# Three edits at once in a latent-attention kernel: ScalarE's order in a loop, the loads of its keys, and the end of a stage

## The chip, the cores and the metric

The kernel runs on one core of a Trainium2 chip. The metric is the device time of one execution in microseconds (us). A core has five engines that run side by side and meet at semaphores: TensorE (PE, matmuls, with its weight loads shown as PEld), VectorE (DVE), ScalarE (ACT), GpSimd (POOL) and SyncE (SP, which here only issues DMAs). Sixteen DMA engines move data between HBM and the core's memory.

## What is computed

Two layers over a small state x (128 tokens of 256 numbers) and a long context `ctx_1024` (12544 tokens of 256 numbers), each of an attention over or fed by the context, an attention among the tokens and a feed-forward part:

```python
x = x + _L0_xattn_ref(_layernorm(x), ctx_1024, ...)   # the "history"
x = x + _L0_attn_ref(_layernorm(x), ...)
x = x + _L0_ffn_ref(_layernorm(x), ...)               # 16 experts, top 2, and a shared one
x = x + _L1_xattn_ref(_layernorm(x), ctx_1024, ctx_1024, ...)
x = x + _L1_attn_ref(_layernorm(x), ...)
x = x + _L1_ffn_ref(_layernorm(x), ...)
```

Two of them see the context, and the change touches only these:

```python
# _L0_xattn_ref: the history is pooled to one vector, from which convolution kernels are made
eh = _gelu(_ln(historical_data @ hist_W + hist_b, hist_ln_g, hist_ln_b))
aw = softmax(_gelu(eh @ ctx_W1 + ctx_b1) @ ctx_W2 + ctx_b2, axis=1)
cc = jnp.sum(eh * aw, axis=1)
kp = _gelu(_ln(cc @ kg_W1 + kg_b1, kg_ln_g, kg_ln_b)) @ kg_W2 + kg_b2
# _L1_xattn_ref: 16 heads of 16 numbers; keys and values are the context times Wq
scores = jnp.einsum('blhe,bshe->bhls', qp, kp)
attn = jax.nn.softmax(scale * scores, axis=-1)
out = jnp.einsum('bhls,bshd->blhd', attn, vp)
```

## The kernel before, in words

**History loop (some 20 to 403 us).** The context goes through in 49 chunks of 256 tokens (`NCH`, `CH`). Each engine runs its own loop over the chunks n, in an order written out by hand; semaphores join them. For chunk n TensorE (loop behind L724) does in turn: the first half of the product with `hist_W` (`project(n, 0)`, L647), the mean square of chunk n - 1 (L673), the transposes of the keys n - 1 for the values (`values_turn`, L722), the second half of the product, the spreading of chunk n - 1's deviations over all rows (`spread_rstd`, L681), in odd chunks a logit product (L705), a half of the hidden product (L696), and the key product of chunk n (`keys_product`, L647, into bank 7). Products with 32-bit data are split in high and low parts.

ScalarE (loop at L1279) does in chunk n: in odd n the hidden's Gelu (`hide_act`, L1216), the key's copy with bias into `k_full` for n - 1 (`keys_full`, L1253), the squares of the first half (`squares(n, 0)`, L1231), the high part of the input n + 1 (`high_part`, L1210), the values' copy (`values_copy`, L1263), the copy of the spread deviations (`widen`, L1238), `squares(n, 1)`, and two features, Gelu with scale and bias (`features`, L1223). In n = 15, 23, 31, 39 and 47 the exponentials of a finished group (`weights`, L1244, group = (n - 15) / 8) take the place of the features; the two features left over come in the next chunk, ahead of its own two (`group_before`, `feature_pair`). Exponentials and Gelu are of different tables of ScalarE; what changes a table is an ACT_TABLE_LOAD. Copies and squares need none.

VectorE makes the high and low parts of the keys (`keys_parts`), adds squares, normalises, and forms the weighted sums. SyncE stores keys and values to HBM: `k_scratch` is an array of 2 (high, low) by 256 by 12544 numbers.

**The history's end (some 403 to 444 us).** VectorE works through the last weighted sums, forms the pooled vector and spreads it (`cc_wide`, L1659). Then it waits until all keys and values are stored, and sets `history_done` (L1664): the memory of the history may now be written over. ScalarE waits for it ahead of `kT` and `v0` (L1318), SyncE ahead of the loads of `rows0` and the experts' weights. VectorE then builds `q_blocks` (L1687), and takes the layer statistics of the product `kg1`. TensorE: the turn of `xn1`, the products to `qkv0`, `kg1` (five products on `cc_wide`), the 16 scores on `q_blocks` and `kT` (L797), the transpose of `kg_h` (L803).

`stay_awake(n, bank)` (L759) is n products of the identity with itself, the results of which nobody reads.

**The context attention (some 548 to 870 us).** Eight pairs of heads s, each with 25 units of 512 keys. `k_stack[s % 2]` holds the keys of a pair: for each head hh of the two, at rows 64 hh: 16 rows high, 16 rows low, one row of ones, 16 rows high. TensorE first finds each unit's maxima (`maximum`, L985; it waits for the chunk's loads), some 28 units ahead of the scores (L1009) and the sums over the values (L1024); VectorE reduces the maxima (L1893), ScalarE takes the exponentials (L1401). The keys come by `load_keys(s, c)` on SyncE's queue in 7 chunks of 1792 keys, six DMAs each, of 16 rows of 7168 bytes. The queue's order: after `x1` two loads of a row of ones (L611) and the keys of pair 0; after `x3` the values of pair 0, ones, the keys and values of pair 1; then for each pair keys and values, a chunk as soon as the scores of pair s - 2 are through with it.

Of the kernel before, what the change touches and what calls it, by code (L numbers as in the profile page):

```python
# [19 lines left out]
F32 = mybir.dt.float32  # L20
# [12 lines left out]
HD = D // H  # L33
# [146 lines left out]
DVE_STEPS = """  # L180
hist_constants hist_weights x_parts mask var1 xn1 g_shift cc_wide history_done q_blocks0 var_kg kg_n att0_0 att0_1
kg_hT att0_2 att0_3 kern_shift kernels s_max0 s_max2 s_max1 probT0 s_max3 probT1
# [83 lines left out]
def build_kernel(nc, k_scratch, v_scratch, ones_scratch, ctx_t, x_in, mask_in, const_in, hist_in, l0_in, rows0_in, xw_in, x_bo_in, x_o_in, l1_in, rows1_in, v_in,  # L266
                 tables_in, out):
    with ExitStack() as outer:
# [265 lines left out]
        def _(sp):  # L534
# [54 lines left out]
            def load_keys(s, c):  # L589

                cols = slice(c * CHUNK, (c + 1) * CHUNK)
                if s >= 2:
                    sp.wait_ge(c_sc, exp_at[EU * (s - 2) + ((c + 1) * CHUNK - 1) // UK][0] + 1)
                for at, which in ((0, 0), (HD, 1), (2 * HD + 1, 0)):
                    for hh in range(2):
                        row = 2 * HD * s + HD * hh
                        sp.dma_start(k_stack[s % 2][64 * hh + at:64 * hh + at + HD, cols].bitcast(F32),
                                     k_scratch[which, row:row + HD, cols]).then_inc(c_stack[s % 2][c], 16)

# [43 lines left out]
        def _(pe):  # L643
# [134 lines left out]
            pe.wait_ge(ld_l0, 16 * L0_PIECES)  # L778
            pe.wait_ge(h_nm, CT * NCH)
            turn("xn1", xn, "xn1_t")  # L780
            act_s.wait(pe, "xT1")
# [6 lines left out]

            pe.wait_ge(ld_kg, 16)
            dve_s.wait(pe, "cc_wide")  # L790
            kg1, kg2 = part(w0, L0_COLS, "kg1", CT), part(w0, L0_COLS, "kg2", KD)
# [183 lines left out]
            def maximum(m):  # L975
# [6 lines left out]
                if u == 0 or (hi - 1) // CHUNK > (lo - 1) // CHUNK:  # L982
                    pe.wait_ge(c_stack[s % 2][(hi - 1) // CHUNK], 96 * (s // 2 + 1))
                for hh, at in enumerate(max_banks(m)):
# [205 lines left out]
        def _(act):  # L1190
# [44 lines left out]
            def widen(n):  # L1235
                act.wait_ge(h_bc, n + 1)
                wait_at(act, h_nm, CT * n)
                A(rstd_wide[:, :], bank[:, 4, 0:CH], ACT.Copy).then_inc(h_rw, 1)  # L1238
# [40 lines left out]
            for n in range(NCH):  # L1279
                if n % 2 == 1 and 0 <= (n - 7) // 2:  # L1280
                    hide_act((n - 7) // 2)
                if 1 <= n:
                    keys_full(n - 1)
                squares(n, 0)
                if 1 <= n and n + 1 < NCH:
                    high_part(n + 1)
                if 1 <= n:
                    values_copy(n - 1)
                    widen(n - 1)
                squares(n, 1)  # L1290
                if group_before(n - 1) is not None:
                    feature_pair(n - 1)
                if group_before(n) is not None:
                    weights(group_before(n))
                else:
                    feature_pair(n)
# [197 lines left out]
        def _(dve):  # L1494
# [164 lines left out]
            done(V.tensor_copy(cc_wide[:, :, :], cc[:, :].unsqueeze(2).broadcast_to([P, CT, P])), "cc_wide")  # L1659
            for b in range(2):  # L1660
                dve.wait_ge(k_stored[b], 32 * ((NCH + 1 - b) // 2))
                dve.wait_ge(v_stored[b], 16 * ((VG + 1 - b) // 2))
            dve.wait_ge(pe_s.sem, 1)
            done(V.memset(gone[:, :], 0.0), "history_done")  # L1664

# [33 lines left out]
            head_blocks(q_blocks, bank[:, 1, 0:T], 0)  # L1699
            head_blocks(q_blocks, bank[:, 1, T:2 * T], 1, "q_blocks0")  # L1700
            pe_s.wait(dve, "kg1")
            layer_stats("_kg", bank[:, 0, 0:D])
# [356 lines left out]
```

## Time and profile before

| | us |
|---|---|
| timed runs | 928.0, 930.33, 933.86 (median 930.33) |
| the profiled execution | 921.35 |
| its span, first to last instruction | 919.6 |
| TensorE busy | 853.1 |
| VectorE busy | 632.9 |
| ScalarE busy | 549.5 |

The profile is of one execution, with a time of its own. The span is what its rows are told in; around it lie 1.75 us. A row of a timeline has the start, the duration, the engine, the line of the kernel, the operation, what it writes and reads, and in brackets how long the engine had stood still and who released it.

### The profile page before, as it was taken

What the parts mean: (1) busy time and instruction counts of PE and PEld (TensorE: products, weight loads), DVE (VectorE), ACT (ScalarE), POOL (GpSimd) and SP (SyncE); (2) the same over time, 40 slices, a digit from 0 to 9 for tenths busy, and PEclk for the clock granted to TensorE, in tenths of its full rate; (3) what the DMA queues carried; (4) which work ended last, traced back from release to release, by engine and by line L of the source; (5) the groups of instructions that cost most, each with busy time, mean ns of one, the idle gap of its engine ahead of it and who ended that gap; (6) DMA issues with size and microseconds to landing.
All of it is one profiled execution on the core that took longest, in us unless ns stands there. A gap on an engine that the chain in (4) does not pass through costs nothing. (4 is left out here: it accounts for less than half of the span.)

```text
span 919.6 us, 21802 instructions
## 1 busy us (share of the span) xinstructions
PE 853.1 (93%) x8804; PEld 690.0 (75%) x8804; DVE 632.9 (69%) x1289; ACT 549.5 (60%) x947; POOL 104.1 (11%) x116
## 2 busy tenths in 40 slices
PE   3999999999999999995889989999999999999988
PEld 3988888887878878864686963677777777778776
DVE  3555666676767767778883449997799999892253
ACT  1776777687686786783731110465577777677521
POOL 1322222222222222200000000000000000000000
PEclk9999999999999999996999999998799999999988
DMA  3376365456546635607608559479698999925100
GB/s 126 105 165 174 106 178 145 140 135 159 144 139 152 150 107 144 164 24 149 278 1 133 83 135 174 116 131 192 118 206 199 163 213 201 156 88 172 62 1 7
DMA packets 83141, 125.01 MB, mean 136 GB/s; under 512 B 10776, under 2 KB 73498, under 8 KB 82268
## 3 DMA queue, kind: packets, MB, share of 16 engines
q1 hardware_dynamic: 83040, 123.61, 56.6%
q8 instruction: 70, 1.15, 0.6%
q14 instruction: 31, 0.25, 0.1%
HBM read 84.06 MB, written 39.52 MB: 134 GB/s over the span
## 5 line engine op out<-in xcount | busy, mean ns | idle before, releaser
L1893 DVE TENSOR_REDUCE unit_max<-bank 128x1 f32<-128x512 f32 (+1 forms) x350 | 221.2, 675 | 29.3 <-PE bank L985 27.6
L1401 ACT ACTIVATE prob<-bank 128x1024 f32<-128x1024 f32 (+1 forms) x200 | 190.8, 1005 | 84.5 <-PE bank L1009 83.9
L647 PE MATMUL bank<-hc_high,w_high 128*128 128x256 f32 x392 | 117.6, 300 | 8.6 <-POOL hc_low L1461 8.4
L1558 DVE SCALAR_TENSOR_TENSOR normed<-bank,b_centered,rstd_wide 128x256 f32<-128x256 f32 x196 | 85.4, 477 | 48.3 <-ACT rstd_wide L1238 48.1
L1024 PE MATMUL bank<-prob,vals 128*32 128x128 f32 x3136 | 110.8, 281 | 3.8 <-issue 2.7
L1009 PEld LDWEIGHTS bank<-q_stack,k_stack 49*128 49x128 f32 x1568 | 105.2, 192 | 11.0 <-ACT q_stack L1393 3.2
L647 PE MATMUL bank<-hc_high,w_low 128*128 128x256 f32 x392 | 112.9, 288 | 0.0
L647 PE MATMUL bank<-hc_low,w_high 128*128 128x256 f32 x392 | 112.6, 287 | 0.0
L1009 PE MATMUL bank<-q_stack,k_stack 49*128 49x128 f32 x1568 | 105.3, 272 | 2.3 <-ACT q_stack L1393 1.1
L985 PE MATMUL bank<-k_stack,q_max 49*128 49x512 f32 (+1 forms) x400 | 100.9, 498 | 2.8 <-DVE unit_max L1893 2.7
L1024 PEld LDWEIGHTS bank<-prob,vals 128*32 128x32 f32 x3136 | 82.4, 112 | 26.9 <-issue 21.9
L1231 ACT ACTIVATE square<-bank,b_centered 128x256 f32<-128x256 f32 x196 | 82.0, 472 | 28.8 <-PE bank L647 28.8
L696 PE MATMUL bank<-eh,hw 128*128 128x512 f32 (+1 forms) x200 | 92.2, 585 | 0.5 <-ACT eh L1223 0.5
L647 PEld LDWEIGHTS bank<-hc_high,w_high 128*128 128x128 f32 x392 | 76.6, 195 | 9.4 <-issue 9.4
L647 PEld LDWEIGHTS bank<-hc_high,w_low 128*128 128x128 f32 x392 | 76.8, 196 | 0.0
L647 PEld LDWEIGHTS bank<-hc_low,w_high 128*128 128x128 f32 x392 | 76.4, 195 | 0.0
L1223 ACT ACTIVATE eh<-normed,hw 128x512 f32<-128x512 f32 (+1 forms) x100 | 74.5, 806 | 0.1
L647 PE MATMUL bank<-hc_high,x_high 128*128 128x256 f32 x196 | 73.2, 373 | 0.0
L985 PEld LDWEIGHTS bank<-k_stack,q_max 49*128 49x128 f32 x400 | 38.3, 187 | 42.9 <-DVE unit_max L1893 19.5
L1582 DVE CUSTOM_DVE_ANT_0 eh<-eh,logits 128x1024 f32<-128x1024 f32 (+1 forms) x52 | 59.5, 1161 | 14.7 <-POOL h_rstd L1466 12.9
L1461 POOL TENSOR_TENSOR hc_low<-hc_raw,hc_high 128x512 fp32r<-128x512 f32 x49 | 62.5, 1275 | 46.4 <-DVE group_stats L1582 45.2
L1536 DVE CAST k_high<-k_full 128x512 fp32r<-128x512 f32 x49 | 20.9, 426 | 64.6 <-ACT k_full L1253 62.5
(324 smaller groups left out, 1339.2 us busy)
## 6 DMA issues: line engine op xcount, KB each, us to landing
k_stack<-k_scratch SPq DMA_DIRECT2D x336, 112.0 KB, 5.4
vals<-v_scratch SPq DMA_DIRECT2D x8, 1666.0 KB, 9.0
v_scratch<-vst SPq DMA_DIRECT2D x12, 1088.0 KB, 10.2
hc_raw<-in_ctx_t SPq DMA_DIRECT2D x49, 256.0 KB, 3.1
k_scratch<-k_high SPq DMA_DIRECT2D x49, 256.0 KB, 3.4
k_scratch<-k_low SPq DMA_DIRECT2D x49, 256.0 KB, 3.5
w_ffn<-in_l SPq DMA_DIRECT2D x4, 1920.0 KB, 14.0
w_l<-in_l SPq DMA_DIRECT2D x6, 603.0 KB, 5.6
```

The lines of the kernel that those rows point to most:

```text
L647: last = nc.tensor.matmul(out_ap, lhs, rhs, start=(n == 0), stop=(n == len(pairs) - 1))
L696: last = nc.tensor.matmul(bank[:, w1_bank(i), 0:width], w1_hist[:, c, :], eh[:, gb, c, at:at + width], start=(c == 0), stop=(c == CT - 1))
L985: last = nc.tensor.matmul(bank[:, at, 0:hi - lo], q_max[head_rows[hh], s, :], k_stack[s % 2][head_rows[hh], lo:hi], start=True, stop=True)
L1009: last = nc.tensor.matmul(bank[:, at + hh, t * T:(t + 1) * T], k_stack[s % 2][head_rows[hh], k * P:(k + 1) * P], q_stack[head_rows[hh], s, ...
L1024: last = nc.tensor.matmul(bank[at:at + 32, SUM_BANK, 0:T], vals[:, s % 2, hh, k * VW:k * VW + 32], prob[:, e % NPB, hh, t * T:(t + 1) * T] ...
L1223: A(eh[:, group % 2, c, at:at + width], normed[:, i % 2, c, 0:width], ACT.Gelu, bias=v_hist["beta"][:, c:c + 1], scale=v_hist["g"][:, c:c ...
L1231: ins = A(square[:, c, :], bank[:, 2 * (n % 2) + half, (c % 2) * CH:(c % 2 + 1) * CH], ACT.Square, bias=b_centered[:, c:c + 1])
L1401: A(prob[:, e % NPB, :, 0:width], bank[:, at:at + 2, 0:width], ACT.Exp).then_inc(c_exp, 1)
L1461: TT(hc_low[:, b], hc_raw[:, b], hc_high[:, b].bitcast(F32), ALU.subtract).then_inc(h_low, 1)
L1558: V.scalar_tensor_tensor(out=normed[:, n // 2 % 2, c, at:at + CH], in0=bank[:, 2 * b + half, (c % 2) * CH:(c % 2 + 1) * CH], scalar=b_cent ...
L1582: V.tensor_tensor_reduce(part_of, part_of, logits[:, gb, lo:lo + width], 1.0, 0.0, ALU.mult, ALU.add, group_stats[:, group, half * CT + c: ...
L1893: V.tensor_reduce(unit_max[:, s % 2, u, hh:hh + 1], bank[:, at[hh], 0:width], AX_X, ALU.max, negate=True).then_inc(c_red, 1)
```

## The change

ScalarE's order in the two iterations behind the exponentials, and where the Gelu's table is loaded. In the first of them (`one_past`) a Gelu of one column comes before `widen`, and `keys_full(n)` of the chunk itself comes between the left-over and the own features. In the second (`two_past`) the values' copy, the high part and `widen` come before both squares, and `keys_full(n)` again before the features. So the two following iterations begin without their `keys_full`:

```diff
-                if 1 <= n:
+                one_past, two_past = (group_before(n - past) is not None for past in (1, 2))
+                if 1 <= n and group_before(n - 2) is None and group_before(n - 3) is None:
                     keys_full(n - 1)
-                squares(n, 0)
-                if 1 <= n and n + 1 < NCH:
-                    high_part(n + 1)
-                if 1 <= n:
+                if two_past:
                     values_copy(n - 1)
+                    if n + 1 < NCH:
+                        high_part(n + 1)
                     widen(n - 1)
+                    squares(n, 0)
+                else:
+                    squares(n, 0)
+                    if 1 <= n and n + 1 < NCH:
+                        high_part(n + 1)
+                    if 1 <= n:
+                        values_copy(n - 1)
+                        if one_past:
+                            A(table_now[:, :], ones[:, :], ACT.Gelu)
+                        widen(n - 1)
                 squares(n, 1)
-                if group_before(n - 1) is not None:
+                if one_past:
                     feature_pair(n - 1)
+                if n + 1 < NCH and (one_past or two_past):
+                    keys_full(n)
```

The keys' loads: for each head the high and low rows in one DMA of 32 rows, the second high rows in one of 16, so four DMAs a chunk. The wait on the chunk's semaphore counts 64 for 96:

```diff
-                for at, which in ((0, 0), (HD, 1), (2 * HD + 1, 0)):
+                for at, which in ((0, 2), (MAX_ROW + 1, 1)):
                     for hh in range(2):
-                        row = 2 * HD * s + HD * hh
-                        sp.dma_start(k_stack[s % 2][64 * hh + at:64 * hh + at + HD, cols].bitcast(F32),
-                                     k_scratch[which, row:row + HD, cols]).then_inc(c_stack[s % 2][c], 16)
+                        row, to = 2 * HD * s + HD * hh, 64 * hh + at
+                        sp.dma_start(k_stack[s % 2][to:to + which * HD, cols].bitcast(F32),
+                                     k_scratch[0:which, row:row + HD, cols]).then_inc(c_stack[s % 2][c], 16)
```

The history's end: VectorE sets `history_done`, with all its waits, behind `q_blocks0` rather than before, and TensorE gets identity products in two places:

```diff
             pe.wait_ge(h_nm, CT * NCH)
+            stay_awake(4, 4)
             turn("xn1", xn, "xn1_t")
...
             pe.wait_ge(ld_kg, 16)
+            stay_awake(8, 4)
             dve_s.wait(pe, "cc_wide")
```

## Rows read from the trace of the kernel before

**Rows 1.** The page, busy time of TensorE: us, share of the span, instructions.

```profile
PE 853.1 (93%) x8804; PEld 690.0 (75%) x8804; DVE 632.9 (69%) x1289; ACT 549.5 (60%) x947; POOL 104.1 (11%) x116
```

**Rows 2.** Waits: engine and line waited for, us in total, times, longest.

```profile
PE bank L722 <- ACT k_full L1253: 8.8, 6, 1.8
...
DVE gone L1664 <- DMA v_scratch<-vst: 1.7, 1, 1.7
```

**Rows 3.** Timeline of TensorE in the history loop, the products that spread deviations (start, duration).

```profile
136.25 0.61 PE L681 MATMUL bank<-const,h_rstd 128*128 128x128 f32 x4
...
146.81 0.85 PE L681 MATMUL bank<-const,h_rstd 128*128 128x128 f32 x4
...
155.21 0.60 PE L681 MATMUL bank<-const,h_rstd 128*128 128x128 f32 x4
...
162.48 0.61 PE L681 MATMUL bank<-const,h_rstd 128*128 128x128 f32 x4
...
330.66 0.61 PE L681 MATMUL bank<-const,h_rstd 128*128 128x128 f32 x4
...
341.09 0.99 PE L681 MATMUL bank<-const,h_rstd 128*128 128x128 f32 x4
```

**Rows 4.** Timeline of ScalarE and TensorE behind an exponential, and in the last chunk.

```profile
136.89 0.38 ACT L1238 ACTIVATE rstd_wide<-bank 128x256 f32<-128x256 f32 x1 [0.83 <-PE bank L681]
...
138.02 1.28 ACT L1223 ACT_TABLE_LOAD   x1
139.32 2.93 ACT L1223 ACTIVATE eh<-normed,hw 128x512 f32<-128x512 f32 x4
142.16 0.67 ACT L1216 ACTIVATE hidden<-bank,hw 128x512 f32<-128x512 f32 x1
142.73 0.82 ACT L1253 ACTIVATE k_full<-bank,x_wts 128x256 f32<-128x256 f32 x2
...
143.60 0.86 PE L722 MATMUL bank<-const,k_full 128*128 128x128 f32 x4 [1.82 <-ACT k_full L1253]
...
400.60 1.98 PE L696 MATMUL bank<-eh,hw 128*128 128x512 f32 x4 [0.54 <-ACT eh L1223]
```

**Rows 5.** Timeline of VectorE and TensorE at the history's end.

```profile
429.12 0.43 DVE L1659 COPY k_full<-cc 128x512 f32<-128x512 f32 x1
...
429.70 2.84 PE L647 MATMUL bank<-w_l,k_full 128*128 128x256 f32 x8 [2.20 <-DVE k_full L1659]
431.29 0.06 DVE L1664 MEMSET gone<- 128x1 f32 x1 [1.73 <-DMA v_scratch<-vst]
...
431.39 2.48 DVE L1687 TENSOR_TENSOR q_blocks<-bank,const 128x1024 f32<-128x1024 f32 x2
...
433.93 5.51 PE L797 MATMUL bank<-kT,q_blocks 128*128 128x128 f32 x32 [0.24 <-DVE q_blocks L1687]
...
439.27 0.38 PE L803 MATMUL bank<-const,kg_h 128*128 128x128 f32 x2
```

**Rows 6.** Windows: stretch, us, busy of each engine, then granted clock, DMA share, GB/s.

```profile
140.00:150.00 10.00, 8.18 (x44) 6.74 (x42) 4.81 (x12) 7.58 (x16) 1.96 (x2) 0.83 0.28 84
...
432.00:434.00 2.00, 1.76 (x5) 0.57 (x3) 1.93 (x3) 1.38 (x2) 0.00 (x0) 0.50 0.74 157
```

**Rows 7.** Windows while the experts' weights load, and while the first keys load.

```profile
436.00:450.00 14.00, 12.29 (x52) 7.58 (x50) 11.12 (x37) 7.52 (x14) 0.00 (x0) 0.95 1.00 426
...
490.00:500.00 10.00, 9.91 (x67) 7.70 (x66) 4.26 (x13) 2.40 (x4) 0.31 (x1) 1.00 1.04 155
```

**Rows 8.** Groups by line and shape: the identity products (busy us, mean ns, idle before).

```profile
L759 PE MATMUL bank<-const 128*128 128x128 f32 x278 | 39.6, 294 | 0.7 <-DVE xT L1941 0.7
```

**Rows 9.** DMA queue in 486.3 to 487.0 (packets, MB, share), SyncE's issue, and `k_stack`'s maxima.

```profile
q1 hardware_dynamic: 1, 0.05, 34.2%
...
485.60 0.54 SPq L611 DMA_DIRECT2D k_stack<-ones_scratch  x2
...
L985 PE MATMUL bank<-k_stack,q_max x400: 379/496/794, 547.8 to 831.6; 49*128 49x512 f32 x128, 49*128 49x256 f32 x6
```

More of the change, by code:

```diff
@@ L180 @@
 DVE_STEPS = """
-hist_constants hist_weights x_parts mask var1 xn1 g_shift cc_wide history_done q_blocks0 var_kg kg_n att0_0 att0_1
+hist_constants hist_weights x_parts mask var1 xn1 g_shift cc_wide q_blocks0 history_done var_kg kg_n att0_0 att0_1
 kg_hT att0_2 att0_3 kern_shift kernels s_max0 s_max2 s_max1 probT0 s_max3 probT1
@@ L982, in maximum @@
                 if u == 0 or (hi - 1) // CHUNK > (lo - 1) // CHUNK:
-                    pe.wait_ge(c_stack[s % 2][(hi - 1) // CHUNK], 96 * (s // 2 + 1))
+                    pe.wait_ge(c_stack[s % 2][(hi - 1) // CHUNK], 64 * (s // 2 + 1))
                 for hh, at in enumerate(max_banks(m)):
@@ L1659, in _ @@
             done(V.tensor_copy(cc_wide[:, :, :], cc[:, :].unsqueeze(2).broadcast_to([P, CT, P])), "cc_wide")
[L1660 to L1664, printed above, removed]
             def layer_stats(n, src):
@@ L1700, in _ @@
             head_blocks(q_blocks, bank[:, 1, T:2 * T], 1, "q_blocks0")
+            for b in range(2):
+                dve.wait_ge(k_stored[b], 32 * ((NCH + 1 - b) // 2))
+                dve.wait_ge(v_stored[b], 16 * ((VG + 1 - b) // 2))
+            dve.wait_ge(pe_s.sem, 1)
+            done(V.memset(gone[:, :], 0.0), "history_done")
             pe_s.wait(dve, "kg1")
```

## The prediction

> **What bounds the kernel now.** I read the page's first part, then the list of waits, then the timeline by stage. TensorE is busy for 93% of a span of 919.6 us [rows 1]: it is the bound, and time can only be won where it stands still, runs at half clock, or where another engine carries a serial stretch. The waits list [rows 2] names such a place in the history loop: the transposes of `k_full` (L722) wait for ScalarE 6 times, 8.8 us in all. The timeline shows where. The products that spread the deviations (L681) come once per chunk and mark its step, in turn 7.3 us (162.48 after 155.21) and 8.15 us (odd chunks also have a logit product). At 136.25 to 146.81 the step is 10.56 us, at 330.66 to 341.09 10.43 [rows 3]; four steps are long so, one behind each of the exponentials of groups 0 to 3 (10.56, 10.77, 9.38, 10.43; first and last shown). The cause is ScalarE's order [rows 4]: a table load of 1.28 us, four features of 2.93 us and the hidden of 0.67 us stand before the copy of `k_full` at 142.73, and TensorE idles 1.82 us for it. It then also drops to half clock (granted 0.83 in 140 to 150 [rows 6]).
>
> The second place is the history's end [rows 5]. VectorE ends the pooled context at 429.12 + 0.43 = 429.55, then `history_done` waits for the last value stores until 431.29, and only then come the two `q_blocks` products, 2.48 us, so that the scores start at 433.93 and the transpose of `kg_h` at 439.27. TensorE's clock is 0.50 in 432 to 434 [rows 6], that is 1.2 GHz, after it had stood still for 2.2 us ahead of 429.70.
>
> The third place does not show as a wait at all: the loads of the keys. No row has TensorE wait for `k_stack`. But the DMA share is 1.04 while they run, at only 155 GB/s; the weights get 426 GB/s at a share of 1.00 [rows 7]. So sixteen engines are full with them.
>
> **ScalarE's order.** In the iteration behind the exponentials the table load (through a one-column Gelu) moves ahead of `widen` (136.89), into its wait of 0.83 us: with the tiny Gelu's own time `widen` comes some 0.6 us late, which VectorE and TensorE have spare. `keys_full(n)` now comes behind two features, not behind four, the hidden and the load: from 142.73 go 0.67, two of the four features (1.46) and the 1.28 less the 0.6 lost, so it starts at some 139.9 and ends at 140.7. TensorE wants it at 143.60 - 1.82 = 141.8. In the next iteration the values' copy, the high part and `widen` come first and the squares after; the squares end some 2 us before the chunk's own key product, ScalarE waits for that with `keys_full` and the features queue behind it by that much; they are wanted two chunks on, so nobody waits. Each long step falls back to 7.29: 41.14 - 4 x 7.29 = 12.0 us; the steps behind them were 0.25, 0, 0.11 and 0.38 late as well. Sum 12.7 us. In the last iteration the load moves likewise, the features end earlier, and TensorE's wait of 0.54 us at 400.60 [rows 4] goes; I count 0.4, since the deviation from GpSimd is the next thing late. Bounds: -13.6 (every idle time of [rows 2] and every half-clock piece) and 0, if the wait only changes its name. The Trainium skill (ScalarE: Activation LUTs, What ACT_TABLE_LOAD costs) puts a table load with its drain at about 2.7 us; the row says 1.28, and that is what I use. By the page `widen` would be 2 us late, and the gain perhaps 1 us less for each.
>
> **The history's end.** `q_blocks` no longer waits for the stores: 429.55 + 2.48 = 432.1, then `history_done`, then ScalarE's `kT` 0.1 + 0.38 later at 432.6 (the stores at 431.29 are hidden behind `q_blocks`; what waits behind `history_done` is `kT`, `v0`, the layer statistics of `kg1` and, 0.8 us later than now in the stage, SyncE's loads of `rows0` and the expert weights, wanted 50 us later). The eight identity products run from 427.5, where `qkv0` ends, to some 429.8 (278 instructions for 139 products, 39.6 us: 0.285 us each [rows 8]) and keep the clock up; `kg1` then takes 2.2 us and ends at 432.0, not 433.5. Were they at half clock they would take 4 us and `kg1` end at 433.2. The scores start at 432.7, run at full clock in 3.9 us (5.51 now, over half of it at 1.2 GHz), so the transpose comes at 436.6, not 439.2: 2.5 us won, the bounds 0.5 and 3. The four products ahead of `xn1`'s turn lie in the wait of 5.2 us for `xT1`: nothing.
>
> Both parts together: 12.7 + 0.4 + 2.5 = 15.6 us.
>
> **The keys.** Six loads a chunk become four; SyncE issues 112 fewer, which is not on the path. Each pair of 16-row loads becomes one of 32 rows whose source is an array of 2 blocks (high, low) by 16 rows by 1792 numbers. What it costs depends on how a load is dealt out to the sixteen engines, and that the rows tell: the loads of one row of ones move as a single packet on a single engine, 0.05 MB in 34.2% of 16 x 0.7 us = 3.83 us, and of the two issued by 486.14 only one moves up to 487.0 [rows 9]; the loads with an outermost count of 16 fill all sixteen (share 1.04). So the outermost count sets the number of engines: one gives one, 16 gives 16. The merged source has an outermost count of 2. Then two engines carry 16 rows each, and where the choice starts from the same engine each time, as for the two rows of ones, they are the same two for every merged load. The Trainium skill says so outright (DMA: Bandwidth & Descriptors, Why a DMA increments its semaphore by 16 and not by 1): the engines are the largest number up to 16 that divides the slowest count of both sides, the lowest-numbered of them, here 2 of 2 and 32. The one-row loads agree; no load of this trace has a count of 2, so this is the step that the rows only bracket. Bounds: zero (dealt by rows), and everything on two engines.
>
> Price of the second: one engine at 426 / 16 = 26.6 GB/s needs 0.269 us for a row of 7168 bytes. In the present loads a row takes 16 x 7168 bytes / 155 GB/s = 0.74 us, as sixteen engines then write to neighbouring rows at once; two engines don't, so I take 0.269 and keep 0.74 as the far end. A chunk gives each of the two 32 rows of the merged loads and 2 of the others: 34 x 0.269 = 9.15 us, a set of 7 chunks 64 us, with its 1666 KB of values (a sixteenth of it each, 4 us) 68 us. Today a set takes (831.6 - 547.8) / 8 = 35 us [rows 9]. So the attention becomes bound by the loads. In the order of SyncE's queue, all 15.6 us earlier: start 485.6 - 15.6 = 470.0; two rows of ones 7.7; set 0 64; values 4; ones 7.7; set 1 64: 617.4. Values 4, then six sets, 6 x 68 - 4 = 404, the last key landing at 1025.4. From the first maxima of the last chunk to the end of the kernel it is today 919.6 - 831.6 = 88 us and three more units of 1.37 us: 92.1. Span 1117.5, with the 1.75 us around it (921.35 - 919.6) 1119.3. That is 197.9 more than the profiled execution. The three timed runs are higher, 930.33 in the median, so I add the difference to that: **1128 us**. The wait is at L985 for `k_stack`; behind it on TensorE stand the scores and the weighted sums, and ScalarE and VectorE wait for those.
>
> **The rivals.**
> - *The rows are spread over all engines* (or over many). Then loads are as now and the 15.6 us remain: 905.8 for the profiled execution, 914.7 as a median: faster by 1.7%. For it: rows of 7168 bytes stay the unit, a merging layer could take the 32 rows of the target as the outermost count, and no wait for keys shows today. Against it: the one-row load, which nothing split.
> - *Two engines, but different ones for the two halves of a chunk.* A chunk then needs 18 x 0.269 = 4.8 us an engine, a set 38 us with its values against 35, and the lead of set 0 and 1 covers most of the rest: some 918 to 925. Against it: the two rows of ones ran one behind the other.
> - *Two engines at today's row price.* 34 x 0.74 = 25 us a chunk, 180 us a set: near 2020. It decides if the write into one row, not the crowd, makes 0.74; the one-row load at 13 GB/s speaks a little for a price between (0.4 us a row would give 1380).
> - *ScalarE's wait at the early `keys_full` takes the place of the old one.* ScalarE has in-order waits there; if features came so late that TensorE waits for them, the gain of the loop falls to 3 or 4 us; with spread loads that gives some 924. Within 1%.
>
> **How the numbers follow.** Two engines at 0.27 to 0.32 us a row: 0.60, own range 1100 to 1230. Two engines and dearer rows: 0.08. Different pairs: 0.04, half of it within 1%, half faster. Spread, gain intact: 0.24. Spread, gain mostly lost: 0.04. To leave out no more than 2 in 10 the range must reach to the spread case: 908 to 1230. Faster by over 1% 0.26, within 1% 0.06, slower by over 1% 0.68 (1% is what a measurement of this kernel can tell from no change; its three runs lie 0.6% apart).
>
> **What would show it.** Right: L722 no longer among TensorE's waits, chunk steps of 7.3 and 8.15 throughout, the table load ahead of L1238; the scores at full clock; in the attention a DMA share near 2/16 with TensorE waiting before L985. Wrong: a share near 1 at 155 GB/s while keys load and no wait at L985 (then the first rival holds); a step over 8.2 us behind an exponential; row times far from 0.27 us.

## The result, and the profile after

The changed kernel takes 1190.62 us in the median of its runs against 929.23 for the kernel before: a ratio of 1.284, 95% interval 1.276 to 1.291. The forecast was 1128 us, in a range of 908 to 1230. Direction and mechanism were right, the size was 63 us too small. The profiled execution took 1201.98 us, with a span of 1200.2. Where a ratio below differs from that of its two medians, it is because the ratio leaves disturbed runs out and the medians don't.

The page of the changed kernel: busy time of the engines, then strips of 40 slices (30 us each) with TensorE's busy share, the granted clock in tenths, the DMA share in tenths and GB/s, then the DMA queue of the loads and the chain that ended last.

```profile
PE 1025.4 (85%) x8828; PEld 824.1 (69%) x8828; DVE 631.2 (53%) x1289; ACT 549.2 (46%) x952; POOL 103.9 (9%) x116
PE   4999999999999798989676877668867888689988
PEclk9999999999999898999655555555565555555697
DMA  3564454555554360131132321312313223130400
GB/s 117 152 166 137 146 155 132 153 158 143 163 143 118 64 263 22 71 110 68 69 110 71 104 79 66 114 70 74 106 69 108 71 71 115 69 109 35 168 2 5
q1 hardware_dynamic: 79680, 123.60, 33.9%
PE 43%; SPq 27%; DMA 19%; DVE 6%; issue 4%; ACT 1%; POOL 0%; POOLq 0%; DVEq 0%; ACTq 0%
```

TensorE was busy 93% of the span [rows 1] and is now at 85%, although its busy time has grown from 853.1 to 1025.4 us: the right half of the clock strip is at 0.5, and the same products take longer there. Below it, in slices 17 to 36, the DMA share is 0.1 to 0.3, where it was 1.04 as the first keys loaded [rows 7]. SyncE's queue and the DMAs hold 46% of the chain.

The waits of TensorE, and the lines on `k_stack` (duration min/median/max in ns, first and last start in us); L987 is what L985 was:

```profile
PE bank L987 <- DMA k_stack<-k_scratch: 126.7, 44, 6.5
...
PE bank L722 <- ACT k_full L1255: 1.5, 2, 1.3
```

```profile
L597 SPq DMA_DIRECT2D k_stack<-k_scratch x224: 302/2382/10310, 472.6 to 1064.4; - x112
...
L987 PE MATMUL bank<-k_stack,q_max x400: 379/760/795, 534.6 to 1099.0; 49*128 49x512 f32 x128, 49*128 49x256 f32 x6
```

126.7 us in 44 waits for keys, of which the kernel before had none; and the maxima run at half clock in the median (760 ns against 496 in [rows 9]). SyncE itself now stands 2.4 us over a key load in the median, up to 10.3, where it was 0.42 before; that fits a full queue. The DMA view of one set's time (700 to 776 us, slices of 1.9 us) shows how the loads run:

```profile
DMA  2211212111331111511211211132111158995111
GB/s 91 66 54 52 92 63 83 61 53 53 94 91 53 53 53 53 136 58 60 79 53 53 91 53 61 53 98 91 53 53 53 53 140 228 353 234 120 53 49 49
...
q1 hardware_dynamic: 1157, 6.34, 26.0%
```

The digit 1 with 53 GB/s is two engines of sixteen (2/16 = 0.125) at 26.5 GB/s each, which is 0.27 us for a row of 7168 bytes. Small rises to 2 or 3 are the 16-row loads; the hill of 5, 8, 9, 9, 5 is the set's values.

The parts in front of the attention, the same views as [rows 4] and [rows 5]; first ScalarE behind the first exponential, then TensorE's spreads of the same chunks and the next, then VectorE and TensorE at the history's end:

```profile
135.74 1.28 ACT L1300 ACT_TABLE_LOAD   x1
137.04 0.20 ACT L1300 ACTIVATE table_now<-ones 128x1 f32<-128x1 f32 x1
137.15 0.36 ACT L1240 ACTIVATE rstd_wide<-bank 128x256 f32<-128x256 f32 x1
...
139.72 0.84 ACT L1255 ACTIVATE k_full<-bank,x_wts 128x256 f32<-128x256 f32 x2
```

```profile
135.92 0.61 PE L681 MATMUL bank<-const,h_rstd 128*128 128x128 f32 x4
...
143.22 0.60 PE L681 MATMUL bank<-const,h_rstd 128*128 128x128 f32 x4
...
151.37 0.61 PE L681 MATMUL bank<-const,h_rstd 128*128 128x128 f32 x4
```

```profile
415.91 0.43 DVE L1673 COPY k_full<-cc 128x512 f32<-128x512 f32 x1
416.37 2.48 DVE L1696 TENSOR_TENSOR q_blocks<-bank,const 128x1024 f32<-128x1024 f32 x2
418.92 0.06 DVE L1714 MEMSET gone<- 128x1 f32 x1
...
416.39 1.99 PE L647 MATMUL bank<-w_l,k_full 128*128 128x256 f32 x8 [1.11 <-DVE k_full L1673]
...
419.61 3.81 PE L799 MATMUL bank<-kT,q_blocks 128*128 128x128 f32 x32 [0.59 <-ACT kT L1332]
423.25 0.38 PE L805 MATMUL bank<-const,kg_h 128*128 128x128 f32 x2
```

The step of 10.56 us is 7.30 (143.22 less 135.92), the copy of `k_full` starts at 139.72 instead of 142.73, the scores take 3.81 us instead of 5.51, and the transpose of `kg_h` comes at 423.25, 16.0 us before its old time. So both other parts did what the forecast said, and the whole loss is behind them.

### The profile page after: what moved, and what is told of

Same layout as the page of the kernel before. It is cut to its first block, busy times and chain, and to the rows that moved or that the text cites. A ratio compares the mean times of both kernels' runs of the same rounds, so it can differ in the third digit from the quotient of the medians.

```text
span 1200.2 us, 21742 instructions
## 1 busy us (share of the span) xinstructions
PE 1025.4 (85%) x8828; PEld 824.1 (69%) x8828; DVE 631.2 (53%) x1289; ACT 549.2 (46%) x952; POOL 103.9 (9%) x116
## 4 chain that ended last, share of the span: by engine, by line
PE 43%; SPq 27%; DMA 19%; DVE 6%; issue 4%; ACT 1%; POOL 0%; POOLq 0%; DVEq 0%; ACTq 0%
SPq L597 26%; DMA k_stack<-k_scratch 19%; PE bank L647 18%; PE bank L696 7%; PE bank L1026 4%; PE bank L1011 4%; PE bank L722 2%; PE bank L681 2%; PE bank L987 2%; PE bank L705 2%; DVE eh L1596 1%; DVE conv L1754 1%; PE bank L673 1%; PE bank L759 1%; SPq L611 1%
## 5 line engine op out<-in xcount | busy, mean ns | idle before, releaser
L987 PE MATMUL bank<-k_stack,q_max 49*128 49x512 f32 (+1 forms) x400 | 144.5, 712 | 128.5 <-DMA k_stack<-k_scratch 126.7
L1011 PEld LDWEIGHTS bank<-q_stack,k_stack 49*128 49x128 f32 x1568 | 180.8, 313 | 12.2 <-issue 4.2
L987 PEld LDWEIGHTS bank<-k_stack,q_max 49*128 49x128 f32 x400 | 59.1, 282 | 180.8 <-issue 172.3
L1026 PE MATMUL bank<-prob,vals 128*32 128x128 f32 x3136 | 181.5, 406 | 0.0
L1011 PE MATMUL bank<-q_stack,k_stack 49*128 49x128 f32 x1568 | 171.5, 386 | 0.2
L1026 PEld LDWEIGHTS bank<-prob,vals 128*32 128x32 f32 x3136 | 129.5, 161 | 45.9 <-ACT prob L1415 26.9
L1233 ACT ACTIVATE square<-bank,b_centered 128x256 f32<-128x256 f32 x196 | 81.4, 472 | 26.5 <-PE bank L647 26.5
L1485 POOL TENSOR_TENSOR rstd<-var_eps,half_power 128x1 f32<-128x1 f32 x8 | 4.4, 549 | 797.3 <-DVE var_eps L1679 793.4
```

The costliest lines, as they stand in the source:

```text
L987: last = nc.tensor.matmul(bank[:, at, 0:hi - lo], q_max[head_rows[hh], s, :], k_stack[s % 2][head_rows[hh], lo:hi], start=True, stop=True)
L1011: last = nc.tensor.matmul(bank[:, at + hh, t * T:(t + 1) * T], k_stack[s % 2][head_rows[hh], k * P:(k + 1) * P], q_stack[head_rows[hh], s, ...
L1026: last = nc.tensor.matmul(bank[at:at + 32, SUM_BANK, 0:T], vals[:, s % 2, hh, k * VW:k * VW + 32], prob[:, e % NPB, hh, t * T:(t + 1) * T] ...
L1233: ins = A(square[:, c, :], bank[:, 2 * (n % 2) + half, (c % 2) * CH:(c % 2 + 1) * CH], ACT.Square, bias=b_centered[:, c:c + 1])
```

## The experiments

All are measured against runs of the kernel before on the same chip (its median 922 to 931 us, each time beside it). Single runs of one kernel scatter by 20 to 40 us, and nearly in line with the mean granted clock of TensorE: the six-load kernel ran 898.4 us at a clock of 0.981 and 934.0 at 0.939. So for the front parts I read stamps of the profile as well. The stretch from one stamp to another repeats to a few tenths from run to run, with one exception: from the first to the last spread of deviations the old order takes 376.3 or 376.4 us in three profiles and 375.0 in `merge_only`, the new one 363.4 or so in all ten.

### The keys

**Six loads again** (`six_loads`). The changed kernel with the old loads and the old wait:

```diff
-                for at, which in ((0, 2), (MAX_ROW + 1, 1)):
+                for at, which in ((0, 0), (HD, 1), (2 * HD + 1, 0)):
...
-                                     k_scratch[0:which, row:row + HD, cols]).then_inc(c_stack[s % 2][c], 16)
+                                     k_scratch[which, row:row + HD, cols]).then_inc(c_stack[s % 2][c], 16)
...
-                    pe.wait_ge(c_stack[s % 2][(hi - 1) // CHUNK], 64 * (s // 2 + 1))
+                    pe.wait_ge(c_stack[s % 2][(hi - 1) // CHUNK], 96 * (s // 2 + 1))
```

> The changed kernel with the six 16-row key loads of the kernel before (and the wait for 96 again): both of the other parts stay. Theory (the whole loss is the merged loads' dealing to two engines): the loss goes completely, the DMA share while keys load is about 1 at 155 GB/s again, no wait for k_stack, and what is left is ScalarE's order (13.3 us by the stamp of chunk 48) and the history's end (2.8 us by the stamp of the kg_h transpose): 912 to 916 us against 929. Rival (the gain in front is given back later, since loads that start earlier meet the weights and TensorE's clock dips longer before the attention: the key loads began only 13.5 us earlier although the transposes of kg_h came 16.0 earlier): 918 to 925 us. Second rival (part of the loss lies elsewhere, such as clock windows at half speed that the change sets off in the attention): over 930 us.

Measured: 913.19 us in the median against 930.57, ratio 0.974 (0.965 to 0.984). No wait for `k_stack` is left. The theory holds: the loss is that of the merged loads, all of it, and what remains of the change is a gain. The forecast had 914.7 us for this case (its first rival).

**The merged loads alone** (`merge_only`): the kernel before with those lines the other way round.

> The kernel before with only the merged loads of 32 rows. Theory (two engines carry the merged loads, and the load queue sets the pace from its start on): the same set period of 76 to 77.6 us as in the changed kernel, everything later by the 13.5 us that the loads start later: 1190.6 + 13.5 = 1204 us, +275 against before. Rival (what bounds is the attention as a whole, with slack between its start and its first wait for a key): as the changed kernel, 1191 us, since an earlier start of the front would not be worth anything once loads bind at the end.

Measured: 1208.33 against 930.57, ratio 1.309 (1.297 to 1.320), with 129.1 us in 47 waits for keys. 1204 was expected; the rival's 1191 is outside. The profiles show why. From SyncE's first key load to the first maxima of the last chunk it is 620.6 us here (484.3 to 1104.9) and 619.5 in the changed kernel (472.6 to 1092.1). So from its start on the load queue sets the pace, and what the front wins is won in the slow kernel too. How much that is stays loose: the medians lie 17.7 us apart, on different chips, the four runs here go from 1199.5 to 1216.0, and this profiled execution is 2.5 us shorter than that of the changed kernel.

**Half of them merged** (`half_merged`): only the first head of a pair.

```diff
+                loads = [(0, 0, 0, 2), (0, MAX_ROW + 1, 0, 1)]
+                loads += [(1, 0, 0, 1), (1, HD, 1, 1), (1, MAX_ROW + 1, 0, 1)]
+                for hh, at, first, blocks in loads:
```

> The changed kernel with only the first head of each pair loaded in one merged load of 32 rows; the second head's stays at 16-row loads. Theory (two engines carry each merged load, row by row at 0.275 us): of a chunk the two engines carry 16 rows of the merged load and 4 of the others, 16 x 0.275 + 4 x 0.44 = 6.2 us, a set of seven chunks 43 us and with its values 47 to 50, so the last key lands near 860 us of the span and the kernel takes 955 to 975 us: a good deal less than half of the loss of 277 us, since the loads have a lead of two sets and the attention's own pace is 35 us a set. Rival (each merged load costs a fixed price of its own in the queue, and half of them half of the loss): 1050 us.

Measured: 1039.94 us, near the rival's number, so my theory's 955 to 975 missed. The DMA view of 700 to 757 us and SyncE's timeline show what was wrong with it:

```profile
DMA  3113185111461118811165211653115557999413
GB/s 101 50 55 105 24 217 115 30 58 49 139 150 46 55 50 206 131 30 50 50 186 116 70 50 67 176 101 111 40 55 158 146 128 186 429 241 226 115 62 106
```

```profile
699.95 45.40 SPq L598 DMA_DIRECT2D k_stack<-k_scratch  x30
745.39 0.84 SPq L605 DMA_DIRECT2D vals<-v_scratch  x1
```

Stretches of 1 (two engines on a merged load) and of 5 to 8 (all on the others) take turns. The next set's values are issued at 805.39, so a set takes 60.0 us. The two busy engines' sum with dearer rows comes to that: 16 rows at 0.27 and the 4 rows of the ordinary loads at the crowd's 0.74 are 7.3 us a chunk, 51 us for seven, and the values some 9 more. The stretches of 1 last 3 to 4 us, as 16 rows at 0.27 do. But the sum was made after the result, and this one run can't tell it from a price that each merged load has of its own, which had the better number. My theory had put the ordinary rows at 0.44 and the set at 50 at most.

**Eight rows** (`eight_rows`): each 16-row load as two of 8.

```diff
+                        for half in range(0, HD, HD // 2):
...
+                            sp.dma_start(k_stack[s % 2][to:to + HD // 2, cols].bitcast(F32),
+                                         k_scratch[which, row:row + HD // 2, cols]).then_inc(c_stack[s % 2][c], 16)
```

> The changed kernel with each 16-row key load cut into two of 8 rows (twelve loads a chunk). Theory (outermost count 8 gives eight engines): the DMA share while keys load is near 8/16. What a row then costs is the open price: if the 0.69 us of a row with sixteen engines is a crowd at one limit of 155 GB/s for all, eight engines need 0.37 us a row, 4.4 us a chunk, and nothing changes in the time (913 us, within 15 for the clock's windows); if it is the price of a row whatever the crowd, a chunk takes 8.3 us, a set 62 us, and the kernel takes near 1080 us. Rival to the theory (eight rows are spread over sixteen engines in halves): the share stays near 1.

**One list of 32 rows** (`one_list`): the scratch is laid out so that the high and low rows of a head follow each other. The loads keep their number, size and target; the target rows come from one list instead of two blocks. The stores become four a chunk.

```diff
-    k_scratch = nc.dram_tensor("k_scratch", (2, D, S), F32, kind="Internal").ap()
+    k_scratch = nc.dram_tensor("k_scratch", (2 * D, S), F32, kind="Internal").ap()
...
-            k_out = k_scratch.rearrange("w (m p) s -> w p m s", p=P)
+            k_out = k_scratch.rearrange("(m g w d) s -> w m g d s", m=KD, w=2, d=HD)
...
-                                     k_scratch[0:which, row:row + HD, cols]).then_inc(c_stack[s % 2][c], 16)
+                                     k_scratch[row:row + rows, cols]).then_inc(c_stack[s % 2][c], 16)
```

> The changed kernel with a scratch in which the 16 high and 16 low rows of a head lie one behind the other (stores go out as four of 8 by 16 rows a chunk instead of two of 128), so that the merged load of the same 32 rows by 1792 has a source that is one list of 32 rows. Theory (the outermost count of the source sets the engines: 2 gave two, 32 gives sixteen): the key loads fill all engines again (DMA share about 1), no wait of TensorE for k_stack, a set in 35 us or less: 905 to 925 us. Rival (a load of 32 rows as such is slow, or loads into 32 partitions from one instruction are): still 1190 us. Second effect to look for: the stores' outermost count is 8, so the eight lower engines would carry them in the history loop; if that bounds the loop, its steps grow over 7.3 and 8.15 us.

Measured: 903.85 us for the one run with eight rows, and 897.56 in the median for the list, against 929.34 (ratio 0.976, 0.968 to 0.984). The DMA views while the first keys load, of the kernel before (488 to 520 us), of the one with eight rows (475 to 500) and of the one with the list (473.5 to 500):

```profile
DMA  9999999899999999999989999999998999996100
...
q1 hardware_dynamic: 1292, 4.63, 95.0%
```

```profile
DMA  3435544445454454545544554445544536553554
...
q1 hardware_dynamic: 1086, 3.94, 49.3%
```

```profile
DMA  6999989999989999999999998999989982000000
...
q1 hardware_dynamic: 1117, 4.83, 84.0%
```

An outermost count of 8 fills eight engines of sixteen (49.3%), 16 and 32 fill all, 2 fills two. The Trainium skill's rule (DMA: Bandwidth & Descriptors, Why a DMA increments its semaphore by 16 and not by 1) fits all four cases. With the list the load is the same 224 KB into the same 32 partitions by the same single instruction as in the changed kernel; only the source's shape differs, and the 277 us are gone. So it is how the source is laid out, and neither the size nor the number of rows. The new layout changes two things at once: the shape (one count of 32 for counts of 2 and 16) and the place in HBM (32 rows one behind the other for two groups far apart). That the shape decides rests on the four counts above; a source of 2 by 16 neighbouring rows, which would separate the two, was not run. The second effect looked for is absent: the last product of the last spread starts at 389.4 us with the list and at 389.5 in the changed kernel, so the stores, whose outermost count is 8, don't bound the loop.

### The parts in front

**ScalarE's order alone** (`order_only`): the kernel before with the new order in the loop and nothing else.

```diff
-                if 1 <= n:
+                one_past, two_past = (group_before(n - past) is not None for past in (1, 2))
+                if 1 <= n and group_before(n - 2) is None and group_before(n - 3) is None:
                     keys_full(n - 1)
...
+                if n + 1 < NCH and (one_past or two_past):
+                    keys_full(n)
```

> The kernel before with only ScalarE's new order in the history loop. Theory: all chunk steps 7.3 and 8.15 us, the spread of chunk 48 at about 389.4 instead of 402.4, and the time 12.5 to 13.3 us below before: 916 to 917 us (ratio 0.986). Rival (the gain in the loop is partly lost at the history's end, where q_blocks then waits for the last value stores, which do not come earlier by as much): 919 to 924 us; the store waits would then be longer than the 1.7 us of before.

Measured: 916.01 against 930.57, ratio 0.978 (0.968 to 0.987).

**The history's end alone** (`end_only`): the kernel before with the later wait and the 4 + 8 identity products.

```diff
+            stay_awake(4, 4)
             turn("xn1", xn, "xn1_t")
...
+            stay_awake(8, 4)
             dve_s.wait(pe, "cc_wide")
```

> The kernel before with only the history's end: later store wait and 4 + 8 identity products. Theory: the scores start some 1.3 us earlier and run at full clock, the transpose of kg_h comes 2.5 to 2.8 us earlier, and the time falls by as much: 926.5 us (ratio 0.997). Rival (the clock has a later dip of its own, which comes earlier or lasts longer when this one is filled): no change, 929 us within 1.

Measured: 928.47 against 930.57, ratio 0.988 (0.975 to 1.001): not told from no change by its time, and the rival isn't excluded by it either. The stamps tell more.

**Without the identity products** (`no_identities`): the six-load kernel less those two lines, so the order and the later wait stay.

> The changed kernel with six key loads and without the 4 and 8 identity products: ScalarE's order and the later store wait stay. Theory A (once ScalarE's order is there the scores run at full clock without help, as in the run of that order alone, and the later wait brings 0.5 to 1 us): the kg_h transpose at 423 to 424 us, as with the products; the time equals that of six_loads within noise, and the half clock behind 452 us is as in the run of the order alone (8 us, not 13 to 14). Theory B (the products are what lifts the clock for the scores): scores over 5 us long again and the transpose at 425 us or later.

Measured: 914.08 against 929.34, ratio 0.981 (0.966 to 0.996). For these parts I take the last spread of the loop (L681's last start) and the last transpose of `kg_h`. In turn: the kernel before, the order alone, the end alone, the kernel without identities.

```profile
L681 PE MATMUL bank<-const,h_rstd x196: 270/275/421, 26.5 to 402.8; 128*128 128x128 f32 x196
...
L803 PE MATMUL bank<-const,kg_h x2: 272/272/273, 439.3 to 439.4; 128*128 128x128 f32 x2
```

```profile
L681 PE MATMUL bank<-const,h_rstd x196: 270/275/376, 25.7 to 389.1; 128*128 128x128 f32 x196
...
L803 PE MATMUL bank<-const,kg_h x2: 272/272/273, 423.8 to 423.9; 128*128 128x128 f32 x2
```

```profile
L681 PE MATMUL bank<-const,h_rstd x196: 270/275/421, 26.6 to 402.9; 128*128 128x128 f32 x196
...
L805 PE MATMUL bank<-const,kg_h x2: 272/272/273, 436.6 to 436.7; 128*128 128x128 f32 x2
```

```profile
L681 PE MATMUL bank<-const,h_rstd x196: 270/275/376, 26.3 to 389.8; 128*128 128x128 f32 x196
...
L803 PE MATMUL bank<-const,kg_h x2: 272/272/273, 424.5 to 424.6; 128*128 128x128 f32 x2
```

From the spread to the transpose it is 36.6 us before, 34.8 with the order alone, 33.8 with the end alone, 33.8 with both (389.1 to 422.9 in the six-load kernel) and 34.8 with the order and the later wait but no identities. So the parts overlap. With the order alone the 32 scores already run at full clock (275 ns in the median against 320 before) and the last value stores hold `history_done` for 0.6 us instead of 1.7; beside the order, the later wait brings nothing and the identity products 1.0 us. The transpose, at 424.5 us, lies between theory A (423 to 424) and theory B (425 or later); that the scores run at full clock without the identities is A's. Its guess about the half clock later on does not hold (below).

### Are the other loads better than the old ones?

The list had been 16 us under the six-load kernel, by runs on different chips. **The list alone in the kernel before** (`list_only`), **eight rows once more** (`eight_timed`) and **six loads once more** (`six_again`) ran together, **the list once more** (`list_again`) after them; the last three repeat kernels shown above.

> The kernel before with only the 32-row loads from a scratch whose 32 rows of a head are one list (without ScalarE's order and without the history's end). Theory (rows from all sixteen engines, but 112 SyncE issues fewer and 32 rows at a time, are cheaper for the engines, 0.48 us a row instead of 0.64 in the mean, so TensorE's instruction fetches meet less of a crowd and its clock falls less often in the attention): the attention has no standstill of 1.6 us marked issue, the mean clock is 0.965 or more in most runs, and the time 10 to 18 us below before: 912 to 920 us. Rival (the gain of one_list over six_loads, 897.6 against 913.2, was the luck of its runs): 929 us, like before, with clocks from 0.93 to 0.975.

> The eight-row loads once more, timed. Theory of the crowd (a key row needs 0.35 us in the mean with eight engines, 0.64 with sixteen, and the other eight engines stay free for TensorE's instructions): the clock in the attention stays up in nearly all runs, 896 to 904 us. Rival (neither the crowd nor the engines matter to the clock): the same 898 to 934 us, median 913, as the kernel with six loads of 16 rows.

> The kernel with both other parts and six 16-row loads once more, on the same chip and against the same runs of before as the two others of this call, since its scatter (898 to 934 us) is as large as what is to be told apart. Theory of the crowd: median 908 to 918 us, with several runs at a mean clock under 0.965. Rival (no difference between the ways of loading as long as all are wide): the same as the eight-row kernel within 5 us.

> The kernel with the order, the history's end and the 32-row loads from one list once more, against runs of before on the same chip: is it the fastest of the versions, or did it have lucky runs? Its first ratio of medians was 897.6 / 929.3 = 0.966; the kernel with six loads had 913.2 / 930.6 = 0.981 and 908.9 / 922.4 = 0.985. Theory (cheaper rows and fewer falls of the clock): 0.965 to 0.972 again, most runs at a mean clock of 0.965 or more. Rival (all wide loads are alike): 0.980 to 0.986.

| kernel | median | before | ratio, 95% interval |
|---|---|---|---|
| `list_only` | 914.35 | 922.37 | 0.996 (0.992 to 1.000) |
| `eight_timed` | 906.17 | 922.37 | 0.984 (0.978 to 0.989) |
| `six_again` | 908.90 | 922.37 | 0.990 (0.984 to 0.996) |
| `list_again` | 898.12 | 925.36 | 0.983 (0.972 to 0.993) |

Eight rows and six loads lie 3 us apart: the rival holds for them, and the 896 to 904 us expected of eight rows were missed. The list alone is 8 us under before by the medians, less than the 10 to 18 expected, and its interval ends at no change. The two series of the list with the other parts stand at 897.6 and 898.1 us, thirteen runs from 893.8 to 912.8, against 898 to 934 for the six-load kernel (but for the one run told of below). By medians the second is 0.971 of before, inside the 0.965 to 0.972 expected; but the intervals of 0.976 and 0.983 overlap with those of 0.974 and 0.990 of the six-load kernel. The clocks point the same way: of the runs made on one chip, 11 of 12 with the list alone had a mean granted clock of 0.965 or more, 9 of 12 with eight rows, 8 of 12 with six loads, 16 of 30 of before, and 12 of the 13 with the list and the other parts. So the order, the end and the list together have the lowest medians measured and are faster than both kernels; that the list is part of why is likely and not shown.

## Why the forecast was right, and where it was short

**ScalarE's order** was right to a few tenths: 12.7 us forecast, 13.1 with the 0.4 of the last chunk, and the last spread came 13.3 us earlier (402.42 against 389.10 by the timelines). 0.4 us of it are no gain of the loop, whose first spread is at 26.1 instead of 26.5. `widen` came 1.23 us behind the spread where it was 0.64 [rows 3, 4], so 0.6 late as forecast; by the 2.7 us for a load that the Trainium skill gives (ScalarE: Activation LUTs, What ACT_TABLE_LOAD costs) it would have been 2 late, and the measured 1.28 decides. `k_full` came at 139.72, forecast 139.9. The rival of a wait taking the wait's place fell: L722 waits 1.5 us in all, not 8.8, though not nothing as forecast, and no wait in TensorE's list is for features.

**The history's end** was right in its sum and wrong in adding. The forecast gave it 2.5 us beside the order; alone it is worth 2.8, beside the order 1.0, while the order is worth 1.8 us more at this place than the loop's own steps. The step that failed is "both parts together: 12.7 + 0.4 + 2.5": two parts were costed on the same half-clock stretch and the same late stores, each as if the other weren't there. The errors cancelled: 16.0 us at the transpose, forecast 15.6.

**The start of the keys** came at 472.04 instead of 470.0. Between the transpose and there TensorE falls to half clock, behind two ScalarE waits of 1.5 and 1.0 us. Windows of 440 to 480 us (us, busy and count, clock, DMA share, GB/s), before, and then after:

```profile
440.00:480.00 40.00, 34.57 (x210) 0.96 0.30 126
```

```profile
440.00:480.00 40.00, 35.14 (x206) 0.87 0.06 18
```

So some 2.5 us are given back. Four profiles without the order have 0.91 to 0.96 here, ten with it 0.83 to 0.96, eight of them at 0.87 or less; no run separates what makes it so. It isn't the identities, without which it was 0.83.

**Two engines** was right, and so was their price: 0.269 us a row forecast, 0.27 measured. The rivals on the dealing and on dearer rows in the merged loads fell with the strip of 53 GB/s. The reason given for the choice, that sixteen engines write to neighbouring rows and two don't, was tested by no run; the price itself was measured.

**The price of a set** is the step that was mis-sized: "64 us, with its values 68". The values are issued at 527.56 and then every 77.4 us in the mean, up to 1069.25. Of the 76.8 us between 684.62 and 761.38, the merged rows are 7 x 32 x 0.27 = 60.5, by the price just as forecast. The rest is twice as dear: some 16 us for the 14 rows of the ordinary loads and the 16 rows that the values put on each engine, 0.54 us a row, where the forecast had 3.8 and 4 us. The cause is presumably that fourteen other engines write at the same time. How the 16 us divide is not shown. The hill of the values is 9.5 us wide (five slices), not 4, but it is the fourteen engines at work: the share of the two busy ones comes behind the keys in front of it, and the values land only 28 us after their issue. I had measured the crowd's price (0.74) and then let no row pay it. From 472.0 to the first maxima of the last chunk, with the ones, it is 620.1 us (forecast 555.4 from 470): 64.7 us too few. Those maxima no longer wait; the last wait for keys was one chunk before:

```profile
1082.65 0.80 PE L987 MATMUL bank<-k_stack,q_max 49*128 49x512 f32 x2 [4.27 <-DMA k_stack<-k_scratch]
...
1092.09 0.79 PE L987 MATMUL bank<-k_stack,q_max 49*128 49x512 f32 x2
```

**The tail**: from there to the end 108.1 us, forecast 92.1. The forecast took it from a kernel at full clock. Windows from the last maxima to the last product over the values, of the kernel before, the changed kernel, and the one with the merged loads alone:

```profile
831.60:867.60 36.00, 34.58 (x741) 1.00 0.44 148
```

```profile
1099.00:1147.00 48.00, 47.79 (x741) 0.68 0.32 111
```

```profile
1109.00:1145.00 36.00, 34.70 (x739) 1.00 0.43 148
```

The same products take 12 us more in the changed kernel. TensorE had been at 0.52 in 1000 to 1099, where it was busy 76.42 of 99 us, and the clock came back late. That is no fixed price of the starved attention: with the merged loads alone TensorE was as starved (0.56 in 1010 to 1109, busy 74.05), yet its clock was back before the last maxima, and from the first maxima of the last chunk (1104.88) to the end it took 92.8 us, as forecast. What decides when the clock comes back is open. Start 2.0, sets 64.7 and tail 16.0 make the 82.7 us by which the span of 1200.2 lies over the 1117.5 forecast. The median of the runs is 11 us below the profiled one, where before it was 9 above, hence only 63 by the medians. What was mis-sized in both kernels with merged loads is the price of the sets; the 16 us of the tail are of this one execution.

## What to carry to other kernels

Fewer and larger loads can be far slower. What counted here is the outermost count of the source: 2 blocks of 16 rows went to two engines and cost 277 us, the same 32 rows as one list went to sixteen and cost nothing, by a different order of the axes in the scratch alone. And gains that rest on the same stall or the same half-clock stretch aren't added: measure each also beside the other.

## What the runs showed beyond that

**A row's price hangs on how many engines load at once.** In the DMA views above, 16 x 32 us x 95.0% over 4.63 MB / 7168 B = 646 rows is 0.75 us a row with sixteen engines; 16 x 25 x 49.3% over 550 rows is 0.36 with eight; the merged loads paid 0.27 with two. In stretches that are full from end to end, sixteen engines moved 157 GB/s (490 to 514 us) and eight 163 (477 to 500): half the engines do all the work. The list, sixteen engines too but 32 rows an instruction, paid 0.53 us a row and moved 220 GB/s (474 to 494), so the count of engines alone doesn't set it. A DMA share near 1 thus didn't mean that all sixteen were needed. What the common limit is stays open.

**Where the scatter comes from.** TensorE's clock falls in the attention at moments that differ from run to run, for 8 to some 50 us. In the profiles of two kernels, before and the order alone, one fall comes at the same instruction, behind a standstill for which no producer is late. TensorE in the kernel before, and the window behind:

```profile
639.03 1.30 PE L1024 MATMUL bank<-prob,vals 128*32 128x128 f32 x20 [1.59 <-issue]
```

```profile
638.00:656.00 18.00, 16.97 (x192) 0.53 0.58 105
...
620.00:636.00 16.00, 15.79 (x296) 1.00 1.04 227
```

In the order alone it stands from 622.64 to 624.23. The DMA queue in 621 to 623 us has one packet of instructions there:

```profile
q1 hardware_dynamic: 85, 0.31, 101.0%
q8 instruction: 1, 0.02, 4.9%
```

4.9% of 16 x 2 us are 1.57 us for one packet among full engines. That TensorE's next instructions came late through the crowd fits this, and the same place in the run of the end alone, where no such standstill shows, has a clock of 1.00 over 620 to 656. It was argued, not tested. The kernel without identities has such a standstill too, 1.61 us ahead of 638.68 at another instruction, with a clock of 0.53 behind it. Against it as the cause of every fall stands the profile of `eight_timed`: no standstill marked issue in the whole attention, and yet 0.50 from 584 to 620 us. And eight rows, which leave half of the engines free, did not lower the median by more than 3 us. Nor was a cause found for one run of the six-load kernel at 2004 us and one of before at 1586, both at full clock, nor for one of before at 1193 with a mean clock of 0.637.
